# Second attention of a two-layer transformer with experts: GpSimd's order in a job, SyncE's load and the out-projection's slot

## The reference, cut to what matters

```python
q = rms_norm((x @ Wq.T).reshape(b, 128, 16, 128), q_norm_w)      # 16 heads of 128
kv_in = concatenate([ctx, x], axis=1)                            # 256 keys
k = rms_norm((kv_in @ Wk.T).reshape(b, 256, 4, 128), k_norm_w)   # 4 key heads
v = (kv_in @ Wv.T).reshape(b, 256, 4, 128)
q, k = rope(q, draft_positions), rope(k, all_positions)
probs = softmax(q @ k.T / sqrt(128))                             # keys repeated 4 times
x = x + (probs @ v).reshape(b, 128, 2048) @ Wo.T
```

## Time and profile before

| | us |
|---|---|
| median of 3 runs | 3105.5 |
| lowest and highest | 3100.2, 3106.0 |
| the profiled execution | 3106.2 |
| its span in the profile | 3104.4 |
| the second attention in it, first load to last router step | 2019.9 to about 2806 |

### The profile page before, as it was taken

The page is one execution under the profiler, slowest core; times in us unless marked ns, Lnnn a source line. Parts: engine busy times, 40 slices in busy tenths (PEclk is TensorE's granted clock), DMA queues, the critical chain, the costliest instruction groups (busy, mean ns, idle before and its releaser), DMA issues. The chain is left out here.

```text
span 3104.4 us, 57661 instructions
## 1 busy us (share of the span) xinstructions
PE 2848.2 (92%) x16353; PEld 1637.9 (53%) x16354; DVE 1829.6 (59%) x5590; ACT 1703.5 (55%) x4562; POOL 1741.2 (56%) x2443
## 2 busy tenths in 40 slices
PE   4699999999999969999999999769999999985998
PEld 2366666666666635555555554335444444443665
DVE  4366666666666655444344344458888888863443
ACT  5578777877778732333233223346666666661332
POOL 6467777777777534554444455366666666631222
PEclk9799999999999989999999999889999999997999
DMA  6711121112111153554555456535555545657444
GB/s 241 251 42 56 51 86 48 48 55 79 58 48 55 54 200 120 161 157 125 147 159 151 137 141 186 141 80 113 122 113 123 122 112 122 123 106 286 80 83 70
DMA packets 467529, 360.89 MB, mean 116 GB/s; under 512 B 295520, under 2 KB 366304, under 8 KB 467424
## 3 DMA queue, kind: packets, MB, share of 16 engines
q1 hardware_dynamic: 404912, 282.85, 32.1%
q0 software_dynamic: 16496, 37.79, 6.3%
q10 hardware_dynamic: 46016, 38.99, 4.4%
HBM read 186.23 MB, written 110.39 MB: 96 GB/s over the span
## 5 line engine op out<-in xcount | busy, mean ns | idle before, releaser
L1393 POOL TENSOR_TENSOR e_st<-e_st,e_ws_tile 128x1024 f32<-128x1024 f32 x64 | 123.8, 1935 | 428.1 <-PE e_y L1149 417.2
L752 ACT ACTIVATE a_nrm<-a_mm,a_sc_t 128x128 f32<-128x128 f32 x768 | 290.8, 474 | 123.6 <-POOL a_sc_t L905 123.4
L603 DVE BATCH_NORM_STATS2 a_st<-a_mm 128x6 f32<-128x128 f32 x768 | 170.7, 285 | 289.5 <-PE a_mm L440 206.5
L439 PE MATMUL a_mm<-a_w_hi,a_xq_hi 128*128 128x512 f16 x768 | 296.6, 386 | 22.7 <-POOL a_xq_lo L887 15.7
L1187 ACT ACTIVATE e_hh<-e_ha 128x512 f16<-128x512 f32 x128 | 76.3, 596 | 411.7 <-PE e_ha L1134 410.1
L440 PE MATMUL a_mm<-a_w_hi,a_xq_lo 128*128 128x512 f16 x768 | 296.4, 386 | 0.0
L1282 DVE SCALAR_TENSOR_TENSOR e_hl<-e_ha,e_hh 128x512 f16<-128x512 f32 x128 | 88.4, 691 | 351.6 <-ACT e_hh L1187 351.2
L904 POOL TENSOR_TENSOR a_sc_t<-a_sc_t,a_mhalf 128x4 f32<-128x4 f32 x192 | 203.2, 1058 | 119.0 <-DVE a_sc_t L610 118.7
L1147 PE MATMUL e_y<-e_w2h,e_hh 128*128 128x512 f16 x640 | 242.6, 379 | 0.0
L1148 PE MATMUL e_y<-e_w2l,e_hh 128*128 128x512 f16 x640 | 242.6, 379 | 0.0
L1149 PE MATMUL e_y<-e_w2h,e_hl 128*128 128x512 f16 x640 | 242.6, 379 | 0.0
(11 more groups left out here) (366 smaller groups left out, 8246.6 us busy)
## 6 DMA issues: line engine op xcount, KB each, us to landing
e_st<-in_w SPq DMA_DIRECT2D x128, 512.0 KB, 4.2
disp<-a_empty SPq DMA_DIRECT2D x16, 2084.0 KB
e_st<-in_w1b SPq DMA_DIRECT2D x32, 352.0 KB, 3.1
disp<-a_empty SPq DMA_DIRECT2D x4, 2605.0 KB, 22.8
e_xb<-disp SPq DMA_DIRECT2D x40, 260.5 KB, 4.3
e_xb<-disp ACTq DMA_DIRECT2D x40, 260.5 KB
a_cx<-in_ctxT SPq DMA_DIRECT2D x32, 256.0 KB, 3.3
a_stage<-in_wprojT SPq DMA_DIRECT2D x16, 512.0 KB, 4.7
```

The lines of the kernel that those rows point to most:

```text
L439: pe.matmul(out, xq_hi[:, n, c, :], w_hi[:, t, c, :], start=(c == 0), stop=False)
L752: ins = act.activation(nrm[:, n % 2, i * P:(i + 1) * P], src[:, i * P:(i + 1) * P], ACT.Identity, bias=sc_t[:, n % 2, 3, i:i + 1], scale=s ...
```

## The change

Four plans get other offsets or another order, and `scales` and `normalise` are edited:

```diff
@@ SyncE
-            run_pipeline(sp, [("in", 5, x_turn), ("job", 2, q_turn), ("att", 3, p_turn), ("end", 7, store), ("end", 2, residual), ("in", 1, x_load)],
+            run_pipeline(sp, [("in", 0, x_load), ("in", 5, x_turn), ("job", 2, q_turn), ("att", 3, p_turn), ("end", 8, store), ("end", 2, residual)],
@@ TensorE
-                              ("att", 5, pv), ("att", 6, out_project), ("end", 11, r_transpose), ("end", 13, r_logits),
+                              ("att", 5, pv), ("att", 7, out_project), ("end", 11, r_transpose), ("end", 13, r_logits),
@@ DVE
-            run_pipeline(dve, [("end", 7, final), ("att", 2, row_scale), ("att", 1, smax), ("job", 2, q_low), ("in", 5, x_low),
+            run_pipeline(dve, [("end", 8, final), ("att", 2, row_scale), ("att", 1, smax), ("job", 2, q_low), ("in", 5, x_low),
                                ("att", 3, p_low), ("job", 0, stats), ("job", 1, v_low), ("att", 5, o_low),
-                               ("end", 7, r_stats), ("in", 3, x_stats), ("end", 14, r_scores), ("end", 16, r_inverse),
+                               ("end", 8, r_stats), ("in", 3, x_stats), ("end", 14, r_scores), ("end", 16, r_inverse),
@@ ScalarE, normalise
                 act.wait_ge(sem["rsum"], at(job, NN1, b))
+                act.wait_ge(sem["scal"], at(job, NN1, b))
@@ GpSimd, scales
+                pool.wait_ge(sem["rot"], at(job, NN1, b))
+                pool.tensor_tensor(r1[:, n, :, :], r1[:, n, :, :], r2[:, n, :, :], ALU.add).then_inc(sem["rsum"], 1)
                 pool.tensor_tensor(c[1], c[0], half[:, 0:4], ALU.pow).then_inc(sem["scal"], 1)
-                pool.wait_ge(sem["rot"], at(job, NN1, b))
-                pool.wait_ge(sem["scal"], at(job, NN1, b))
-                pool.tensor_tensor(r1[:, n, :, :], r1[:, n, :, :], r2[:, n, :, :], ALU.add).then_inc(sem["rsum"], 1)
@@ GpSimd
-            run_pipeline(pool, [("in", 2, c_low), ("job", 0, scales), ("in", 3, x_scale), ("in", 5, tables), ("end", 8, r_scale),
+            run_pipeline(pool, [("in", 2, c_low), ("job", 0, scales), ("in", 3, x_scale), ("in", 5, tables), ("end", 9, r_scale),
```

## The result

| | before, us | changed, us |
|---|---|---|
| median | 3104.7 | 3078.2 |
| lowest and highest | 3100.2, 3106.0 | 3075.3, 3079.8 |
| the profiled execution | 3106.2 | 3075.3 |
| a steady round, mean of the eleven of the earlier trace rows | 46.5 | 44.8 |

The ratio is 0.9916, with a 95% interval of 0.9899 to 0.9933: 26.5 us less. The forecast was 3075, or 30.5 us less. (`scales` begins at line 1978 of the kernel before, not at 1976. From line 1875 the changed kernel's numbers are up to one higher than before's, so L1878, L1898 and L1914 are now L1879, L1899 and L1915; in GpSimd's job the sum is L1995 and the power L1996.)

The account below looks back on a forecast made before the run. The loop of DVE, ScalarE and GpSimd was taken as the bound, not TensorE. Twelve steady rounds gave 22.8 us, filling rounds 4.4, drain 3, last round 0.3: 30.5 less, so 3075 us, range 3062 to 3094 (8 in 10).

Parts of the forecast that it names:

- The pace: Second attention, steady rounds: the loop of DVE, ScalarE and GpSimd sets 46.5 us a round; TensorE, with 43.3 of work, follows.
- The load: Context load issued in slot 0 instead of slot 1: ScalarE's late start in slot 2 goes, 1.6 us a round, bounds 1.3 to 2.1.
- The round without a load: Last round of the trace before, taken as clean: slot 3's maximum to output low half 5.52 us, against 7.37 with a load.
- The sum: GpSimd's sum ahead of its power: 0.3 us a round gained, between -1.0 and +1.4, with moved meetings netting 0.
- The out-projection: Out-projection, final sum, store and router statistics one slot later: 0 in steady rounds, TensorE's stops of 3.2 us a round lose their reason.
- the drain: End of the stage, after the steady rounds: the later out-projection and final sum save 3 us, between 0 and 5.
- (a): Rival: TensorE becomes the bound as the loop drops below its 43.3 us; each round gives 3.2, so 3058; chance 0.1.
- (b): Rival: another wait replaces the load's, ScalarE on DVE's reciprocal or a returning router meeting; 0.47 us a round, 3100; chance 0.1.
- The router's meeting: DVE's small router instruction held up by GpSimd's context low half in four of twelve rounds: 1.20 us instead of 0.23.
- (c): Rival: slower, the moved sum falls on DVE's two-input instructions in further slots; three more meetings a round give 3119; chance 0.07.
- (d): Rival: the load isn't early, its conditions hold SyncE at slot 0 and turns queue behind; 0 or worse, 3105; chance 0.02.

## Why the prediction was right, and where it wasn't

**The pace.** Right. An engine that waits for DVE, while DVE doesn't wait for it, follows: shown by the cut that removed 24 us of TensorE's work in 500 and no time, and by the same cut's 31 us once TensorE had no stop left. Its work was given as 43.3 us a round; without any stop it is 42.8. TensorE's busy time gives 43.3 too, before (512.19 of 550) and changed (483.18 of 500), so half a us of what the profile counts as busy wasn't needed; where it sits stays open.

**The load.** Right in mechanism. 1.6 us a round was forecast; alone, the load took the round from 46.5 to 45.1, 1.4, near the lower of the bounds worked out. For the whole the term was 12 x 1.6 + 4.4 = 23.6 us, and 19 were measured. In company it is worth more: 37 us in the changed kernel (1.0036 against 0.9916), in part because the out-projection's move costs less once the load is early. The round without a load was a good witness for the step itself (5.52 forecast, 5.60 measured), less good for the round.

**The sum.** Alone the term had the wrong size and sign: 0.3 us a round were to come, and 0.1 were lost. Its parts came in part as worked out: slot 1's stop is 1.25 us where 1.2 was said, and in slot 2 the sum met a small instruction (L1743, 0.72 for 0.17 us) and not the low half beside it. But alone it took away every meeting of the probability low halves, slot 1's too, which was to shrink by 0.4 only. That all the moves of meetings cancel was close for the sum alone. In company it was wrong: with load and out-projection the order is worth 17 us, and the conversion L1808 is 0.66 us a round shorter, 9 us over 14 rounds. The prediction looked at four large places where the sum can fall, and not at that one of two elements a partition. With the conversion set apart, the 0.3 us a round of the working is what is left in three of the four pairs of the table.

**The out-projection.** This is the step that failed: "DVE keeps all its instructions: the final sum leaves slot 3 (0.6 us sooner maximum) and comes back in slot 4", costed at nothing. The question that was not asked is whether slot 3's 0.6 us were on the path. They stood ahead of a stop that lasts until ScalarE is ready, so they were free; slot 4's are not. Alone, the move costs 18 us; the router's statistics, which go with it, push the conversion into the sum and make the other half of that. That TensorE's two stops would go and give nothing was right. In the changed kernel nothing of this cost is left: the load has taken slot 3's stop away, so the final sum was on the path in either place, and the sum's order has taken the meeting away. There the move gives 7 us, and the final sum still costs 0.8 us a round that a place in a stop would save.

**The sum of terms.** 30.5 us forecast, 26.5 measured, but not by those terms. So the total that came near is in part luck. By the ratios the three edits alone make -19, +3 and +18, which is 2 us slower together. What makes -26 of it is that they suit each other: the out-projection's move costs 8 us less with the early load, 10 less with the sum first, and the rest comes only with all three; each of these is uncertain by some 8 us or more, and the rounds say the same with 0.6, 0.8 and 0.3 us each. The range, too, took ends for the sum of -0.5 and +0.8 where its working had -1.0 and +1.4, with no reason given. In the two profiles the eleven rounds of the earlier trace rows give 18.7 us (46.53 against 44.83), where 1.9 x 11 = 21 was forecast. From the stage's first load to the start of these rounds it is 2176.60 - 2016.06 = 160.5 us, not 2189.84 - 2019.86 = 170.0: 9.4 us, against 4.4. The last round lost 0.7, and the stretch from there to the last output low half gave 1.1, against 3 for the drain: its final sum waits 1.35 us, not 2.87, but the last output low half still stops for 4.00. Another 3.8 us between the two profiles lie ahead of the stage, where nothing was changed, and 1.4 are lost behind its last output low half; together that is the 30.9 us between the two spans.

**The rivals.** (a) came true, but only for a kernel that wasn't forecast: with the high half first the loop drops below TensorE's work. (b) came in its first half: ScalarE in slot 2 waits for DVE's reciprocals, 1.08 us in the round shown. Its price was wrong, as the gain of the load stayed. The router's meeting (L1793) didn't return. (c) in its own form, the moved sum falling on more two-input instructions, didn't come. A meeting did decide the kernels with only one of sum and out-projection, but with a conversion of one input, and with the power first it was the conversion that had moved, not the sum. (d) left no trace.

## What to carry to other kernels

Ask of each instruction that is moved not only what it costs, but whether it stood in front of a stop: work ahead of a wait for another engine is free until the wait is gone, and the same work behind it is paid in full. Where an engine stops, look at what the engine that it waits for did in between, and whether all of it had to come first; a high half whose input was ready long ago, queued behind a chain, was worth 27 us here on top of all three edits. Edits of order don't add: measure them in company before one is dropped or kept.

## What the runs showed of the hardware

How small an instruction can be and still be held up by GpSimd's sum was unexpected. DVE's conversion of 128 by 2 numbers, one input, lasted 0.81 us for 0.17, ending with the sum that had begun before it, and a multiplication of 128 by 4 numbers lasted 0.72 for 0.17. The prediction spoke of instructions with two inputs in SBUF only. The Trainium skill (SBUF — State Buffer, Who interferes with whom) does list casts and tensor_scalar among the operations that can take the shared ports, and has who issued first hold them for the whole instruction; the traces agree, and here the price per meeting is what is left of the sum, 0.3 to 1.0 us. The size of the one that is held up doesn't enter: the conversion lost 0.65 us, and the normalised low half of 128 by 512 at 2372.09 lost 0.32 (1.01 for 0.69, beside a sum from 2371.28 to 2372.55).
